# Unread products on TensorE in the idle times around the routing stage of a transformer layer

## The chip, the core and the metric

The kernel runs on one core of one Trainium2 chip. The metric is the device time of one execution in microseconds (us), from start to end of the program on that core. The kernel before takes 848.81 us, the median of three runs (846.87, 848.81 and 850.23). TensorE has two clock levels, 1.2 and 2.4 GHz. The profile shows the granted one as a share of the upper level, 0.50 or 1.00 (a mean over a stretch can lie between).

## What is computed

One transformer layer on x of 8 blocks x 512 rows x 256 features, in fp32: attention with 16 heads and a bias by relative position, then a mixture of seven routed experts (two per row) and one shared expert.

```
x = x + attention(layernorm(x))        # softmax(q k / 4 + bias) v, then Wo
y = layernorm(x)
sh = gelu(y @ sw1 + sb1) @ sw2 + sb2
topv, topi = top_k(y @ gate_w.T + expert_bias, 2); w = softmax(topv)
routed = sum over the two chosen e of w_e * (gelu(y @ rw1[e] + rb1[e]) @ rw2[e] + rb2[e])
out = x + sh + routed
```

## The kernel before

The program has three stages, each a block in which every engine has its own list of instructions; a block ends for all engines together. Inside a block the order of each engine's work is written out by hand, and semaphores (`wait_ge`, `then_inc`) tie the engines to each other.

`project` (L254) makes q, k and v of the eight blocks. `attend` (L573) runs 32 slots of four heads each. Its PE list computes scores for the row maxima (L800), exponents (L817, L825) and the values (`values`, L830, products at L839 into `pC`). The last thing that PE does in it is `values` of slot 31 (L860, L861). In the same stage DVE ends with two context products (`context`, L566, L570), which wait for loads of the context and of the inverse denominators and release the output projection through `c_ready`; ACT copies the last `pC` to `ctx_sb` (L775) and SP stores it.

`finish` (L864) has the rest, in three parts. In the routing part (PE: L1647 to L1670) a loop goes over the eight blocks b. `out_projection(b)` (L1520, L1528) makes the attention's output in `pX[:, 1]`, DVE adds the residual (L1134) and takes the statistics, POOL makes the inverse deviation (L1081, L246 to L251), ACT normalises the rows into `xr` (L1411), and PE turns them (`turn_rows`, L1532, L1538), makes the gate product (`gate`, L1544) and turns the logits into `pX[:, 0, 1]` (`turn_logits`, L1550). DVE copies them out (L1156, which counts `lg_done`), chooses the experts and makes ranks and slots (L1221 to L1229) out of `rank`'s products (L1553), and POOL scatters the rows to `routed_rows` by eight indirect DMAs for each block (L1099). Interleaved with this is the shared expert: `shared_up` (L1589), `turn_shares` (L1580), ACT's copy to `cTs` (L1437), `shared_down` (L1602, L1604) and DVE's `add` (L1238). The block of the loop runs b = 0 to 7, and the shared expert of blocks 0 to 4 (`EARLY` is 3) is done by the end of the part.

Between the parts (PE: L1671 to L1683, "the gap" in what follows) DVE works out a table of tiles (L1241), SP writes padding rows (L1021) and, once all scatters have landed, loads the first eight tiles of 256 rows (L1040). PE meanwhile does the shared expert of blocks 3 and 4. In the expert part (L1684 on) PE takes 38 tiles: `turn_tile` (L1614), `expert_up` (L1626), `expert_down` (L1637); DVE scales the results and POOL scatters them (L1115). Then the last three blocks of the shared expert and the sums follow.

`ident` is the 128x128 identity, `wo_f` the output projection's weights in fp32, both in SBUF from before the end of the attention on (`small_ld` counts eight loads, the last of them issued at about 480 us). `pS`, `pU`, `pD` and `pX` are PSUM banks. An fp32 product shows as two records of PE in the trace.

Of the kernel before, what the change touches and what calls it, by code (L numbers as in the profile page):

```python
# [20 lines left out]
B, S, D = 8, 512, 256  # L21
# [4 lines left out]
NI = HG * B  # L26
# [43 lines left out]
SMALL = 8  # L70
# [26 lines left out]
def raw(t):  # L97

    return t.bitcast(F32)
# [10 lines left out]
def layer_kernel(nc, x, wqT, wkT, wvT, woT, rel_emb, gateT, expert_bias, w1, b1, w2, b2, low_rows,  # L110
# [22 lines left out]
    with top:  # L133
# [32 lines left out]
        with ExitStack() as ctx:  # L166

            sb, _, sem = mk(ctx)
            near = sb("near", [P, 2, HPG, TW], F32)
            bandT = sb("bandT", [P, 2, HPG // 2, 2, BW], F32R)  # L170
            q_st = sb("q_st", [P, RING, HPG // 2, S], F32R)
            k_st = sb("k_st", [P, RING, HPG // 2, S], F32R)
            v_raw = sb("v_raw", [P, RING, TT * HPG * DH], F32)
            near_ld = [sem(f"near_loaded{j}") for j in range(HPG)]
            band_ld = [sem(f"band_loaded{j}") for j in range(HPG)]
            qk_ld = [sem(f"qk_loaded{r}") for r in range(RING)]
            far_ld = [sem(f"far_loaded{r}") for r in range(RING)]
            v_ld = [sem(f"v_loaded{r}") for r in range(RING)]
            rows_set = sem("rows_set")
            qk_out = [sem(f"qk_out{m}") for m in range(4)]  # L180
            v_out = sem("v_out")
            loads = attention_loads(locals())
            scope = locals()
            project(nc, mk, scope)
            attend(nc, mk, scope)
# [384 lines left out]
    dve.tensor_tensor(cn[:, b % 2], cn[:, b % 2], rb[:, b % 2], ALU.mult).then_inc(g["c_ready"], 1)  # L570


def attend(nc, mk, g):  # L573


# [6 lines left out]
    with ExitStack() as ctx:  # L582
# [8 lines left out]
        pS = ps("pS", [P, 3, S], F32)  # L591
        pE = ps("pE", [P, 4, S], F32)
        pC = ps("pC", [P, S], F32)
        s_mm, max_done, split_done, max_turned, max_out, max_ld = (sem(n) for n in (
            "s_mm", "max_done", "split_done", "max_turned", "max_out", "max_loaded"))
# [3 lines left out]
        PV0, MAX0 = 8, 4  # L599
# [12 lines left out]
        with nc.Block() as block:  # L612
# [174 lines left out]
            def _(pe):  # L787
# [42 lines left out]
                def values(n, par, t, first=False):  # L830

                    if t == 0:
                        pe.wait_ge(exp_done, STEPS * n + STEPS)
                        pe.wait_ge(v_ready, n + 1)
                        if not first:
                            pe.wait_ge(evac, n)
                    for j in range(HPG):
                        at = 8 * (j // 2) + 2 * t + j % 2
                        ins = pe.matmul(pC[32 * j:32 * j + 32], v_aug[:, par, t, j], prob[:, par, at],  # L839
                                        start=t == 0, stop=t == TT - 1, skip_group_check=True)  # L840
                    ins.then_inc(pv_done, 1)
# [17 lines left out]
                        slot(4 * quad + u, u, quad, first=quad == 0, last=quad == QUADS - 1)  # L859
                for t in range(TT):  # L860
                    values(NI - 1, 1, t)  # L861


def finish(nc, mk, g):  # L864
# [3 lines left out]
    passed, ident = g["passed"], g["ident"]  # L868
    ctx_dram, rden_dram, xs_dram, yc_dram = g["ctx_dram"], g["rden_dram"], g["xs_dram"], g["yc_dram"]
    wst, x1, wo_f, ga_f, eb, b1s, b2f, b2_low, ctx_sb = (  # L870
        g[n] for n in ("wst", "x1", "wo_f", "ga_f", "eb", "b1s", "b2f", "b2_low", "ctx_sb"))
    cn, rb, w_sh, x1c, route = g["cn"], g["rb"], g["w_sh"], g["x1c"], g["route_sb"]
    wst_ld, x_ld, small_ld = g["wst_ld"], g["x_ld"], g["small_ld"]
    c_ready, route_ld, x_late, pad_out = g["c_ready"], g["route_ld"], g["x_late"], g["pad_out"]
    with ExitStack() as ctx:
# [70 lines left out]
        def down_of(b, t2):  # L946
            return pX[:, 0, t2].rearrange("p (u d) -> p u d", u=2) if b == OWN else pD[:, t2]

        def hidden_of(b):
            return cn[:, 0] if b == OWN else h_f  # L950

        def shares_of(b):
            return hT[0:3 * NE, 0, 0] if b == OWN else cTs

        def last_user(b):
            return b - 2 if b > OWN else b - 1
# [17 lines left out]
        pU = ps("pU", [P, 2, S], F32)  # L974
        pD = ps("pD", [P, 2, 2, D], F32)
        pX = ps("pX", [P, 2, 2, S], F32)
# [6 lines left out]
        s = {n: sem(n) for n in names}  # L983
# [11 lines left out]
        with nc.Block() as block:  # L995
# [523 lines left out]
            def _(pe):  # L1519
                def out_projection(b):  # L1520
                    pe.wait_ge(c_ready, b + 1)
                    for t2 in range(2):
                        if b >= 1:
                            pe.wait_ge(s["x1_add"], 2 * b - 1 + t2)
                        for u in range(2):
                            t = 2 * t2 + u
                            for c in range(MC):
                                ins = pe.matmul(pX[:, 1, t2, D * u:D * u + D], cn[:, b % 2, c, t:S:TT], wo_f[:, c],  # L1528
                                                start=c == 0, stop=c == MC - 1)
                        ins.then_inc(s["wo_mm"], 1)  # L1530

                def turn_rows(b):  # L1532
                    pe.wait_ge(s["xn1"], 4 * b + 4)
                    if b >= 1:
                        pe.wait_ge(s["r_done"], b)
                    for c in range(MC):
                        for t in range(TT):
                            ins = pe.transpose(pX[:, 0, c, P * t:P * t + P], xr[:, b % XR, t, 0, P * c:P * c + P], ident[:])  # L1538
                        ins.then_inc(s["xT2_mm"], 1)
# [30 lines left out]
                def turn_shares(b):  # L1570
                    pe.wait_ge(s["comb_done"], 3 * b + 3)
                    if b == TILES_FROM:
                        pe.wait_ge(s["ev_done"], 2 * NT)
                    if b == OWN:
                        pe.wait_ge(s["xlo"], NT)
                    elif b >= 1:
                        pe.wait_ge(s["sh_acc"], 2 * last_user(b) + 2)
                    flat = down_of(b, 1)[0:3 * NE].rearrange("p u d -> p (u d)")
                    for t in range(TT):
                        ins = pe.transpose(flat[:, P * t:P * t + P], raw(combine_p[:, b % CB, t]), ident[:])  # L1580
                    ins.then_inc(s["c_turn"], 1)

                def shared_up(b, m):
                    if b == TILES_FROM:
                        pe.wait_ge(s["hhi"], 2 * NT)
                    if b >= 1 and b != OWN:
                        pe.wait_ge(s["h_done"], 2 * last_user(b) + m + 1)
                    for c in range(MC):
                        ins = pe.matmul(up_of(b, m), w_sh[:, 0, c, P * m:P * m + P], x2T(b)[:, c],  # L1589
                                        start=c == 0, stop=c == MC - 1)  # L1590
                    ins.then_inc(s["u_mm"], 1)

                def shared_down(b, halves=(0, 1)):
                    pe.wait_ge(s["b2_split"], 2)
                    pe.wait_ge(s["h_done"], 2 * b + 2)
                    pe.wait_ge(s["cT_done"], b + 1)
                    if b >= 1 and b != OWN:
                        pe.wait_ge(s["sh_acc"], 2 * last_user(b) + 2)
                    for t2 in halves:
                        for u in range(2):  # L1600
                            t = 2 * t2 + u
                            pe.matmul(down_of(b, t2)[:, u], shares_of(b)[:, P * t:P * t + P], b2s[:], start=True, stop=False)  # L1602
                            for m in range(2):
                                ins = pe.matmul(down_of(b, t2)[:, u], hidden_of(b)[:, m, P * t:P * t + P], w_sh[:, 1, m],  # L1604
                                                start=False, stop=m == 1)
                        ins.then_inc(s["d_mm"], 1)
# [40 lines left out]
                pe.wait_ge(small_ld, 16 * SMALL)  # L1647
                out_projection(0)
                out_projection(1)
                turn_rows(0)  # L1650
                pe.wait_ge(s["consts"], 8 + NE)
                pe.wait_ge(s["tri_done"], 1)
# [21 lines left out]
                pe.matmul(pX[:, 1, 0, 0:2 * NE], ones_b[:], cum[:, B], start=True, stop=True).then_inc(s["cnt_mm"], 1)  # L1674
                shared_up(EARLY + 1, 1)
                shared_down(EARLY)
                turn_shares(EARLY + 1)
                shared_down(EARLY + 1)
                pe.wait_ge(s["tab_done"], 2)
                pe.wait_ge(s["r_done"], B)  # L1680
                pe.wait_ge(s["h_done"], 2 * TILES_FROM)
                pe.wait_ge(s["sh_acc"], 2 * TILES_FROM)
                pe.wait_ge(s["w_lo"], 2 * NR)  # L1683
                experts = ()  # L1684
                for k in range(-3, NT):
                    if k + 3 < NT:
# [110 lines left out]
```

## Time and profile before

| | us |
|---|---|
| median of three runs | 848.81 |
| lowest and highest | 846.87, 850.23 |
| the profiled execution | 853.25 |
| its span, first to last instruction | 851.4 |
| PE busy in it | 785.6 (92%) |
| DVE busy | 620.7 (73%) |
| ACT busy | 477.5 (56%) |
| POOL busy | 252.5 (30%) |
| mean granted clock of TensorE | 0.943 |

The span starts with the first instruction; all times of rows are counted from there. The attention stage ends at about 523 us, the routing part at about 655, the gap at about 678, the expert part at about 812. Matmuls are pipelined, so the last record of a group overlaps the next group by some tenths of a microsecond. "Idle before" in a timeline stands in square brackets with what ended it.

### The profile page before, as it was taken

Reading aid. Unit: us, or ns where it says so; the run is one execution under the profiler, and the core shown is the slowest. Engines: PE = TensorE matmul, PEld = TensorE weight load, DVE = VectorE, ACT = ScalarE, POOL = GpSimd, SP = SyncE. Lnnn points to the kernel's source line nnn. Section 1 sums busy time; section 2 is a strip of 40 time slices with the busy share of each in tenths; the row PEclk is TensorE's granted clock in tenths of the full one; section 3 lists DMA queues with packets and bytes.
Section 4 is the critical chain, followed back from the end, with each engine's and each line's share of the span. In section 5 each row is a group of like instructions: output and inputs, shape, how many; then the busy total and the mean of one; then the engine's idle time right before and its main releaser. Section 6 shows DMA issues by size and latency. Waiting matters only on the chain. (4 is left out here: it accounts for less than half of the span.)

```text
span 851.4 us, 18147 instructions
## 1 busy us (share of the span) xinstructions
PE 785.6 (92%) x6177; PEld 543.4 (64%) x6177; DVE 620.7 (73%) x1928; ACT 477.5 (56%) x720; POOL 252.5 (30%) x407
## 2 busy tenths in 40 slices
PE   4999889999999999999999997688878799999996
PEld 2777646666666666666656555455553499999954
DVE  5666588888888888888888832576765367667854
ACT  2444306666666666666666672465553177777720
POOL 1122011111121112111211110277776145655530
PEclk9999959999999999999999998699898689999998
DMA  4999894543564335443444813455513625556676
GB/s 118 279 350 355 281 221 106 161 116 94 131 167 133 95 106 169 131 117 114 125 138 135 278 61 126 153 185 181 165 71 101 189 84 150 168 158 206 199 259 235
DMA packets 74631, 140.75 MB, mean 165 GB/s; under 512 B 14520, under 2 KB 34640, under 8 KB 74366
## 3 DMA queue, kind: packets, MB, share of 16 engines
q1 hardware_dynamic: 62962, 116.91, 45.7%
q0 software_dynamic: 9792, 19.54, 7.0%
q10 hardware_dynamic: 1788, 3.18, 1.1%
q8 instruction: 49, 0.80, 0.4%
q14 instruction: 40, 0.33, 0.1%
HBM read 85.71 MB, written 56.78 MB: 167 GB/s over the span
## 5 line engine op out<-in xcount | busy, mean ns | idle before, releaser
L734 DVE CUSTOM_DVE_ANT_0 sums<-pS,near 128x512 bf16<-128x512 f32 x512 | 329.4, 687 | 47.7 <-PE pS L800 39.0
L767 ACT ACTIVATE prob<-pE 128x1024 f32<-128x1024 f32 x256 | 248.4, 1022 | 148.3 <-PE pE L825 148.3
L825 PEld LDWEIGHTS pE<-bandT,place 64*128 64x128 f32 x2048 | 166.1, 189 | 12.6
L825 PE MATMUL pE<-bandT,place 64*128 64x244 f32 (+2 forms) x2048 | 163.3, 271 | 0.0
L800 PE MATMUL pS<-k_st,q_st 48*128 48x512 f32 x512 | 138.3, 476 | 6.1 <-DMA k_st<-k_parts 3.5
L839 PE MATMUL pC<-prob,v_aug 128*32 128x512 f32 x1024 | 135.7, 604 | 1.0 <-ACT ctx_sb L775 1.0
L800 PEld LDWEIGHTS pS<-k_st,q_st 48*128 48x128 f32 x512 | 62.6, 192 | 115.2 <-DVE nmax L734 88.3
L817 PE MATMUL pE<-q_st,k_st 62*128 62x512 f32 x512 | 114.9, 406 | 2.0 <-issue 1.9
L1115 POOL DMA_INDIRECT expert_rows<-rb,xr x76 | 77.3, 1017 | 75.9 <-DVE rb L1328 61.3
L1099 POOL DMA_INDIRECT routed_rows<-xr,slot_i x64 | 65.2, 1019 | 33.4 <-issue 19.3
L1637 PE MATMUL pD<-w2p,hT 128*128 x456 | 63.8, 289 | 2.0 <-DVE hT L1321 1.6
L817 PEld LDWEIGHTS pE<-q_st,k_st 62*128 62x128 f32 x512 | 57.1, 188 | 8.4 <-ACT prob L767 5.0
L703 POOL DMA_DIRECT2D q_st<-negated_maxima x64 | 34.8, 548 | 91.2 <-DMA negated_maxima<-turned 91.2
L1637 PEld LDWEIGHTS pD<-w2p,hT 128*128 128x128 f32 x456 | 56.8, 190 | 2.9 <-issue 2.9
L712 POOL COPY v_aug<-v_raw 128x256 f32<-128x256 f32 x32 | 12.6, 395 | 151.9 <-PE pC L839 151.9
L498 PE MATMUL pQ<-xT,w_p 128*128 128x512 f32 x192 | 49.8, 410 | 2.6 <-DVE xT L409 1.5
L696 POOL DMA_DIRECT2D negated_maxima<-turned x32 | 22.5, 703 | 90.0 <-DVE turned L747 86.0
L1321 DVE TENSOR_TENSOR hT<-ctx_sb,hT 128x512 fp32r<-128x512 f32 x38 | 26.3, 693 | 27.8 <-ACT hT L1467 21.8
L498 PEld LDWEIGHTS pQ<-xT,w_p 128*128 128x128 f32 x192 | 36.2, 196 | 14.0 <-DVE qk L416 4.5
L1604 PE MATMUL pD<-w_sh,ctx_sb 128*128 128x256 f32 x112 | 44.8, 539 | 0.0
L734 DVE DVE_READ_ACCUMULATOR2_ANT nmax<- 128x1 f32 x512 | 42.5, 83 | 0.0
L839 PEld LDWEIGHTS pC<-prob,v_aug 128*32 128x32 f32 x1024 | 20.6, 108 | 32.7 <-issue 30.0
(187 smaller groups left out, 1046.8 us busy)
## 6 DMA issues: line engine op xcount, KB each, us to landing
xr<-routed_rows SPq DMA_DIRECT2D x38, 258.0 KB
q_st<-q_parts SPq DMA_DIRECT2D x64, 128.0 KB, 2.7
k_st<-k_parts SPq DMA_DIRECT2D x64, 128.0 KB, 2.9
ctx<-ctx_sb SPq DMA_DIRECT2D x32, 256.0 KB, 2.8
q_parts<-qk SPq DMA_DIRECT2D x14, 512.0 KB, 8.2
k_parts<-qk SPq DMA_DIRECT2D x14, 512.0 KB, 7.6
near<-bias_by_distance SPq DMA_DIRECT2D x16, 448.0 KB, 5.0
xr<-expert_rows SPq DMA_DIRECT2D x14, 512.0 KB, 6.6
```

The costliest lines, as they stand in the source:

```text
L498: ins = pe.matmul(pQ[:, m % 2], w_p[:, a, w, c, P * h:P * h + P], xT[:, par, z, c], start=k == 0, stop=k == 5)
L703: pool.dma_start(raw(q_st[row:row + KM, m % RING]), max_dram[m].rearrange("a (p h) s -> h a p s", h=2)[side]).then_inc(max_ld, 16)
L734: dve.tensor_tensor_reduce(sums[:, r % 4], pS[:, unit % PS], near[:, hg % 2, j, lead:lead + S], -1.0, BIG, ALU.add, ALU.min, nmax[:, j, t: ...
L767: act.activation(prob[:, par, 2 * step:2 * step + 2], pE[:, 2 * (step % 2):2 * (step % 2) + 2], ACT.Exp).then_inc(exp_done, 1)
L800: pe.matmul(pS[:, unit % PS], q_st[rows, r, pair, P * t:P * t + P], k_st[rows, r, pair], start=True, stop=True).then_inc(s_mm, 1)
L817: pe.matmul(pE[:, bank + side], k_st[rows, r, pair, P * t:P * t + P], q_st[rows, r, pair], start=True, stop=False, skip_group_check=True)
L825: ins = pe.matmul(pE[:, bank + side, a:z], place[rows, half], bandT[rows, (quad // 2) % 2, pair, part, lead:lead + z - a], start=False, st ...
L839: ins = pe.matmul(pC[32 * j:32 * j + 32], v_aug[:, par, t, j], prob[:, par, at], start=t == 0, stop=t == TT - 1, skip_group_check=True)
L1099: pool.indirect_dma_start(xs_dram[:, :], bass.IndirectOffsetOnAxis(ap=slot_i[:, b, c, t:t + 1], axis=0), xr[:, b % XR, t, c], None).then_i ...
L1115: pool.indirect_dma_start(yc_dram[:, :], bass.IndirectOffsetOnAxis(ap=place_of, axis=0), y_rows(i)[:, t], None).then_inc(y_out[i % NXG], 16)
L1604: ins = pe.matmul(down_of(b, t2)[:, u], hidden_of(b)[:, m, P * t:P * t + P], w_sh[:, 1, m], start=False, stop=m == 1)
L1637: ins = pe.matmul(pD[:, i % 2, t], hT[:, i % 2, a, TS * m + P * t:TS * m + P * t + P], w2p[:, bass.ds(expert, 1), z, m].rearrange("p a n - ...
```

## The change

A helper `keep_turning` issues `count` fp32 products of `ident` with the first 256 columns of `wo_f` into a given PSUM bank. Nothing reads the results, and no semaphore is counted by them. It is called at five places of PE's list: after the last `values` of the attention (five products into `pS`, behind two waits of its own), after `out_projection(1)` (six into `pU`), after `shared_down(EARLY)` (two into `pX[:, 0, 1]`, behind a wait on `lg_done`), after `turn_shares(EARLY + 1)` (four into the same bank), and behind the waits that stand ahead of the expert part (three into `pU`). Twenty products in all. Nothing is removed or moved.

```diff
@@ -570,6 +570,12 @@
     dve.tensor_tensor(cn[:, b % 2], cn[:, b % 2], rb[:, b % 2], ALU.mult).then_inc(g["c_ready"], 1)
 
 
+def keep_turning(pe, g, bank, count):
+
+    for _ in range(count):
+        pe.matmul(bank, g["ident"][:], g["wo_f"][:, 0], start=True, stop=True)
+
+
 def attend(nc, mk, g):
 
 
@@ -859,6 +865,9 @@
                         slot(4 * quad + u, u, quad, first=quad == 0, last=quad == QUADS - 1)
                 for t in range(TT):
                     values(NI - 1, 1, t)
+                pe.wait_ge(g["small_ld"], 16 * SMALL)
+                pe.wait_ge(max_done, MAX0 + 16 * NI)
+                keep_turning(pe, g, pS[:, 0, 0:D], 5)
 
 
 def finish(nc, mk, g):
@@ -1647,6 +1656,7 @@
                 pe.wait_ge(small_ld, 16 * SMALL)
                 out_projection(0)
                 out_projection(1)
+                keep_turning(pe, g, pU[:, 0, 0:D], 6)
                 turn_rows(0)
                 pe.wait_ge(s["consts"], 8 + NE)
                 pe.wait_ge(s["tri_done"], 1)
@@ -1674,13 +1684,17 @@
                 pe.matmul(pX[:, 1, 0, 0:2 * NE], ones_b[:], cum[:, B], start=True, stop=True).then_inc(s["cnt_mm"], 1)
                 shared_up(EARLY + 1, 1)
                 shared_down(EARLY)
+                pe.wait_ge(s["lg_done"], B)
+                keep_turning(pe, g, pX[:, 0, 1, 0:D], 2)
                 turn_shares(EARLY + 1)
+                keep_turning(pe, g, pX[:, 0, 1, 0:D], 4)
                 shared_down(EARLY + 1)
                 pe.wait_ge(s["tab_done"], 2)
                 pe.wait_ge(s["r_done"], B)
                 pe.wait_ge(s["h_done"], 2 * TILES_FROM)
                 pe.wait_ge(s["sh_acc"], 2 * TILES_FROM)
                 pe.wait_ge(s["w_lo"], 2 * NR)
+                keep_turning(pe, g, pU[:, 0, 0:D], 3)
                 experts = ()
                 for k in range(-3, NT):
                     if k + 3 < NT:
```

## Rows read from the trace of the kernel before

**Rows 1.** The head of the page.
```profile
span 851.4 us, 18147 instructions
```

**Rows 2.** Stretches: start:end, length, busy time of five engines, granted clock, DMA.
```profile
519.70:522.40 2.70, 0.00 (x0) 0.00 (x0) 0.54 (x1) 0.57 (x1) 0.00 (x0) 1.00 0.60 228
522.50:529.20 6.70, 5.64 (x13) 4.60 (x14) 1.28 (x2) 0.00 (x0) 1.17 (x16) 0.50 0.07 20
...
536.20:549.70 13.50, 10.12 (x26) 5.69 (x27) 8.42 (x43) 7.78 (x16) 2.48 (x8) 0.50 0.56 176
...
638.60:645.20 6.60, 6.60 (x13) 3.06 (x14) 2.58 (x4) 3.58 (x8) 5.08 (x6) 0.50 0.32 115
...
665.90:686.20 20.30, 17.18 (x52) 12.57 (x53) 4.72 (x9) 5.42 (x11) 0.00 (x0) 0.50 0.50 140
```

**Rows 3.** Timeline of PE, 515 to 552: start, duration, instructions, idle before, releaser.
```profile
515.98 3.64 PE L839 MATMUL pC<-prob,v_aug 128*32 128x512 f32 x32 [0.98 <-ACT ctx_sb L775]
523.56 10.28 PE L1528 MATMUL pX<-wo_f,cn 128*128 128x256 f32 x32 [3.94 <-PEq L612]
538.04 1.97 PE L1538 MATMUL pX<-ident,xr 128*128 128x128 f32 x8 [4.20 <-ACT xr L1411]
540.78 3.57 PE L1544 MATMUL pX<-x2T,ga_f 128*7 128x512 f32 x4 [0.78 <-ACT x2T L1419]
...
545.64 5.83 PE L1528 MATMUL pX<-wo_f,cn 128*128 128x256 f32 x16
```

**Rows 4.** Timeline of PE, later groups of the same lines.
```profile
560.14 4.00 PE L1528 MATMUL pX<-wo_f,cn 128*128 128x256 f32 x16
...
566.47 1.88 PE L1544 MATMUL pX<-x2T,ga_f 128*7 128x512 f32 x4 [0.74 <-ACT x2T L1419]
...
625.44 1.06 PE L1538 MATMUL pX<-ident,xr 128*128 128x128 f32 x8 [0.41 <-DVE ranks L1221]
...
637.41 1.09 PE L1538 MATMUL pX<-ident,xr 128*128 128x128 f32 x8 [1.85 <-ACT xr L1411]
```

**Rows 5.** Timeline of DVE, 516 to 531.
```profile
521.86 1.23 DVE L570 TENSOR_TENSOR cn<-cn,rb 128x1024 f32<-128x1024 f32 x1 [4.04 <-DMA rb<-inverse_denominators]
...
530.14 0.69 DVE L1134 TENSOR_TENSOR x<-pX,x 128x512 f32<-128x512 f32 x1 [2.01 <-PE pX L1528]
```

**Rows 6.** Timeline of POOL, its first indirect DMA of the routing part.
```profile
553.58 1.20 POOL L1099 DMA_INDIRECT routed_rows<-xr,slot_i  x1 [7.77 <-DVE slot_i L1229]
```

**Rows 7.** Timeline of PE, 657 to 689.
```profile
657.32 0.38 PE L1602 MATMUL pD<-b2s,cTs 24*128 24x256 f32 x1
...
661.75 1.13 PE L1604 MATMUL pD<-w_sh,ctx_sb 128*128 128x256 f32 x4
664.40 0.60 PE L1580 MATMUL pD<-ident,combine_p 128*24 128x128 f32 x4 [1.52 <-DVE x1c L1238]
667.36 0.55 PE L1602 MATMUL pD<-b2s,cTs 24*128 24x256 f32 x1 [2.36 <-ACT cTs L1437]
...
675.38 2.08 PE L1604 MATMUL pD<-w_sh,ctx_sb 128*128 128x256 f32 x4
678.55 1.94 PE L1614 MATMUL pX<-ident,xr 128*128 128x128 f32 x8 [1.09 <-DVE x1c L1238]
681.05 2.93 PE L1626 MATMUL pU<-xgT,w1c 128*128 128x256 f32 x12 [0.56 <-DVE xgT L1306]
...
687.16 1.67 PE L1637 MATMUL pD<-w2p,hT 128*128 x12
```

**Rows 8.** Timelines of ACT, DVE and the SP queue, 660 to 681.
```profile
666.52 0.59 ACT L1437 ACTIVATE cTs<-pD 24x512 fp32r<-24x512 f32 x1 [1.63 <-remote]
...
677.50 0.69 DVE L1238 TENSOR_TENSOR x1c<-pD,x1c 128x512 f32<-128x512 f32 x1 [4.26 <-PE pD L1604]
...
672.48 8.12 SPq L1040 DMA_DIRECT2D xr<-routed_rows  x8
```

**Rows 9.** DMA issues of the whole run: count, KB each, median us to landing.
```profile
out<-x1d SPq DMA_DIRECT2D x2, 256.0 KB, 2.0
```

## The prediction, made before the changed kernel ran

> **What bounds the kernel now.** I read the page first, then the granted clock of TensorE by stretches, then PE's timeline in the stretches at half clock, then the timelines of the engines that release PE there.
>
> The span is 851.4 us [rows 1], and PE is the busiest engine in nearly all of it, so its clock matters wherever PE is what comes late. The stretches [rows 2] show when it doesn't run at 2.4 GHz. The last values of the attention end at 519.62, PE stands idle for 3.94 us until the projection at 523.56 [rows 3], and the clock, still 1.00 up to 522.4, is at 0.50 (1.2 GHz) from 522.5 to 529.2. After the two projections PE stands for 4.20 us [rows 3], and the clock is at 0.50 again from 536.2 to 549.7. Between the last sums of the shared expert of block 3 (662.88) and those of block 4 (667.36) PE does only 0.60 us of transposes [rows 7], and the clock is at 0.50 from 665.9 to 686.2. These three pieces hold 40 us at half clock, and the five additions stand in the idle times ahead of, or inside, these pieces. There are other short pieces at half clock, such as 638.6 to 645.2 [rows 2], that nothing of the change touches.
>
> Is PE late in these pieces? From 523.56 on the chain goes projection(0), DVE's sum at 530.14 [rows 5], statistics, POOL's and ACT's normalising, transposes at 538.04, gate product at 540.78, logits, projection(2) to 551.5 [rows 3], ranks, slots, and POOL's first indirect DMA at 553.58, for which it had waited 7.77 us [rows 6]. From there on POOL issues its scatters nearly without rest, so what moves its first one moves the whole routing part; I find nothing in it that hangs on a fixed time, since the context loads, weight loads and scatters are all released from this same chain. In the third piece the shared sums run from 667.36 to 677.46, DVE adds them, and only then does PE turn the first tile, at 678.55 [rows 7, 8].
>
> **The change, part by part.** A product here is the form of the projection: 128x128 stationary, 256 columns, fp32. Its group of 16 records (8 products) takes 4.00 us at full clock [rows 4], so one costs 0.50 us. At half clock 13 records take 5.64 us of busy time [rows 2], 0.87 us a product, and the two products at 675.38 take 2.08 us [rows 7], 1.04 each: 0.87 to 1.04.
>
> Place 1, five products after the attention: 2.5 us, from 519.62 to 522.1. The block can't end before DVE's second context product, 521.86 + 1.23 = 523.09 [rows 5], so they are hidden with 1.0 us to spare. Their waits are for loads issued some 40 us earlier and for maxima long done. PE's idle time shrinks from 3.94 to 1.4 us, and the clock should be full at 523.56. Then projection(0) takes 4.00 us and ends at 527.56 where DVE's sum started at 530.14: 2.6 us gained on the chain.
>
> Place 2, six products after the two projections: these now end at 523.56 + 8.00 = 531.6, and the six at 534.6. The transposes, which wait for ACT, come at 538.04 - 2.6 = 535.4, so the six are hidden with 0.8 us to spare. If the clock stays full, three groups of the chain shorten: transposes 1.97 to 1.06, gate 3.57 to 1.88, projection(2) 5.83 to 4.00 [rows 3, 4], in all 0.9 + 1.7 + 1.8 = 4.4 us. Places 1 and 2 together: 7.0 us, POOL's first scatter at 546.6. What is late next there is DVE's choosing of the experts, which ends before projection(2) and so hides under it.
>
> Here a rule can be weighed. The trace has groups of transposes that differ in the idle time ahead: at 625.44, after 0.41 us of idle, the clock didn't fall; at 637.41, after 1.85 us, it was at 0.50 from 638.6 [rows 2, 4]. In the changed kernel the idle ahead is 0.8, between the two. The Trainium skill (TensorE: Matmul & The Clock Gate, Part 4: PE-mode transpose) says that transposes don't count as busy in the way products do. By that rule the stretch from 534.6 to the gate product is idle as a whole, and the time would be that of the first rival. The row at 625.44 neither shows nor excludes it.
>
> Place 3, two products after the shared sums of block 3: 662.88 to 663.9. The transposes behind them wait for DVE until 664.40 [rows 7]; hidden with 0.5 us to spare. The added wait on the logits' copy is long fulfilled, as all routing is behind it. Place 4, four products behind these transposes: 665.0 to 667.0, while PE stands until 667.36 for ACT's copy at 666.52 [rows 7, 8]; hidden with 0.4 us to spare. ACT's 1.63 us of idle before that copy has no releaser that I can name. If it were absent in some run, the four products would be late by up to 1 us. With the clock kept, the shared sums of block 4 take as long as those of block 3 did, 657.32 to 662.88, 5.56 us in place of 10.1, and end at 672.9.
>
> Place 5, three products, 1.5 us, behind the last waits and directly ahead of the first tile's transposes. The waits were fulfilled 1.09 us after the sums; now that is 674.0, and the three end at 675.5. Is a tile there by then? SP issues the first tile load at 672.48 [rows 8], and transfers of 256 KB land after 2.0 us [rows 9], with seven more queued behind this one and the last scatters just done: 674.5 at the earliest, and 676 if it takes as much again. So the load covers most of the 1.5 us, and without that cover they would cost their full 1.5. The transposes start at 675.5 to 676, in place of 678.55: 3.0 us. The filling of the expert pipeline, 678.55 to 687.16, then runs at full clock: halving 1.94, 2.93 and the following transposes and products (3.3 us until the first down product) [rows 7] gives up to 4.1 us; but ACT's and DVE's steps between these groups don't shorten, and start to show. I take 2.6, with 2.0 and 3.1 as bounds. Places 3 to 5: 5.6 us.
>
> The sum is 7.0 + 5.6 = 12.6 us. The profiled execution took 853.25 us around its span of 851.4; less 12.6 that is 840.6. The median of the runs is 848.81, 4.4 lower than the profiled one, and 848.81 - 12.6 = 836.2. I don't take all of it: the profiled one may hold more time at half clock than the others, for where the clock rises and falls varies. The piece from 665.9 to 686.2 is the likeliest to be shorter elsewhere, since PE was busy in 17.18 of its 20.3 us [rows 2] before the clock rose. I take 2 us off the gain for this and predict 838 us. Past 690 nothing is changed, and the work there hangs on the tiles' progress, so I let the gain reach the end.
>
> **The rivals.** First, the clock is held in only one of the two places. If it falls again around the first transposes, 4.4 us of 12.6 are lost; if in the third piece, 5.6: by the same scaling 838 + 4.4 = 842.4 and 843.6. For it: the stretch between 534.6 and the gate product has 0.8 + 1.06 + 0.78 us with no product. Against: a similar stretch at 625.44 stayed at full clock. Chance 0.25.
>
> Second, the gain is swallowed: POOL's scatters, the loads of context or the expert phase's DMAs turn out to set the end, or an earlier schedule puts the unchanged short idles of the routing part so that the clock falls there more often. Each such piece of 6.6 us at half clock costs up to 3.3 us [rows 2]; three more eat 10: 845 to 852. Against it speaks POOL's wait of 7.77 us before its first scatter. Chance 0.08. That the change doesn't do what it says (products that keep nothing up, yet fit under the waits) gives 848.8: chance 0.03.
>
> Third, slower: the products don't hold the clock, and then cost double just where they stand ahead of waited-for work. At 0.87 to 1.04 us each: five end at 524.0 to 524.8 against 523.56 (0.4 to 1.3 late); six after 533.84 at 539.1 to 540.1 against 538.04 (1.0 to 2.0); two and four 0.3 to 0.6 and 1.1 to 1.9; three ahead of the first tile 2.6 to 3.1. Sum 5.4 to 8.9, so some 856 us. It decides from where the clock is at 0.50 at 523.56 in spite of five products. Against it: at each fall in these rows PE had hardly any product in the 3 us before. Chance 0.04.
>
> **How the numbers follow.** Forecast 838 (834 to 841) 0.60; one place only 0.25; swallowed 0.08; no effect 0.03; slower 0.04. A measurement of this kernel can tell about 0.5%, 4.2 us, from no change: the bounds are 844.6 and 853.1. The first two cases lie below 844.6 but for a tail of 0.02, and most of the swallowed case above it: faster 0.84, same 0.12, slower 0.04. The range takes the forecast's full scaling with the upper bounds of the unknowns (848.8 - 12.6 - 2.5 = 833.7) with 1 us for run-to-run spread below, and the one-place case with a little of the swallowed one above: 833 to 845.
>
> **What would show it.** Granted clock 1.00 from 523 to 550 in the profile after; PE's idle ahead of the projection near 1.4 us with its start still near 523.6; POOL's first scatter near 546.6; shared sums of block 4 in 5.6 us; first tile transposes 3 us after SP's first tile load. A start of the projection later than 523.6, transposes that no longer wait for ACT or DVE, or a clock of 0.50 at these places would prove the step wrong.

## The result

The changed kernel takes 840.05 us, the median of 15 runs (833.45 to 846.43), against 846.87 us for the kernel before in 15 runs (840.16 to 850.54). The ratio is 0.9906, with a 95% interval of 0.9879 to 0.9933: 8.0 us faster, between 5.7 and 10.2. Measured once more on another occasion (below) it was 0.9875 (0.9841 to 0.9910). The forecast was 838 us, 10.8 us below the 848.81 us known then. Ratios, intervals and the means over many runs leave out executions more than 1.5% above the fastest of the same kernel.

The head of the page after, its line of the clock in 40 slices, and the stretches (columns as in [rows 2]):

```profile
span 835.4 us, 18227 instructions
...
PEclk9999959999999999999998999998998999999999
```
```profile
521.00:523.30 2.30, 2.30 (x12) 1.76 (x10) 0.00 (x0) 0.60 (x1) 0.00 (x0) 1.00 0.68 257
525.30:538.00 12.70, 11.07 (x50) 10.39 (x51) 7.16 (x21) 2.09 (x5) 3.39 (x23) 1.00 0.49 128
539.10:542.30 3.20, 3.09 (x4) 0.38 (x4) 1.27 (x2) 1.92 (x4) 1.04 (x2) 0.50 0.56 205
664.00:690.00 26.00, 23.51 (x164) 20.63 (x164) 12.60 (x25) 14.73 (x34) 5.24 (x5) 1.00 0.46 135
```

The projections and the whole third piece run at full clock now, where [rows 2] had 0.50. One short fall is left near the first gate product, 3.4 us in place of the 13.7 us of before. (Lengths of falls are read from the clock's own record; the stretches shown stay some tenths inside them.) PE's timeline at the start of the routing part, against [rows 3]; line numbers are 6 to 10 higher than before, and L576 is the added product:

```profile
520.94 2.43 PE L576 MATMUL pS<-wo_f,ident 128*128 128x256 f32 x10
525.26 7.81 PE L1537 MATMUL pX<-wo_f,cn 128*128 128x256 f32 x32 [1.90 <-PEq L618]
532.91 2.75 PE L576 MATMUL pU<-wo_f,ident 128*128 128x256 f32 x12
537.29 1.09 PE L1547 MATMUL pX<-ident,xr 128*128 128x128 f32 x8 [1.63 <-ACT xr L1420]
539.21 3.46 PE L1553 MATMUL pX<-x2T,ga_f 128*7 128x512 f32 x4 [0.83 <-ACT x2T L1428]
...
543.78 4.11 PE L1537 MATMUL pX<-wo_f,cn 128*128 128x256 f32 x16
```

The five products end 1.90 us before the projection may start, the six end 1.63 us before the transposes may: both hidden. The projections take 7.81 us in place of 10.28. The gate product came at half clock here, 3.46 us. PE had stood 1.63 and 0.83 us on both sides of the transposes; but in e1 below it stood 1.61 and 0.83 us at the same place and the clock stayed up, so these idle times alone don't decide it. In the gap, against [rows 7]:

```profile
660.19 1.03 PE L576 MATMUL pX<-wo_f,ident 128*128 128x256 f32 x4
661.81 0.60 PE L1589 MATMUL pD<-ident,combine_p 128*24 128x128 f32 x4 [0.59 <-issue]
662.24 1.89 PE L576 MATMUL pX<-wo_f,ident 128*128 128x256 f32 x8
664.88 0.35 PE L1611 MATMUL pD<-b2s,cTs 24*128 24x256 f32 x1 [0.74 <-ACT cTs L1446]
...
669.28 1.13 PE L1613 MATMUL pD<-w_sh,ctx_sb 128*128 128x256 f32 x4
671.39 1.53 PE L576 MATMUL pU<-wo_f,ident 128*128 128x256 f32 x6 [0.99 <-DVE x1c L1247]
672.76 0.60 PE L1623 MATMUL pX<-ident,xr 128*128 128x128 f32 x4
673.74 0.66 PE L1623 MATMUL pX<-ident,xr 128*128 128x128 f32 x4 [0.37 <-DMA xr<-routed_rows]
...
678.53 1.67 PE L1646 MATMUL pD<-w2p,hT 128*128 x12
```

The shared sums of block 4 run from 664.88 to 670.41, 5.53 us in place of 10.1, and the second half of the first tile's transposes waits 0.37 us for a DMA: in this trace the loads have become what is late. It isn't so in every trace (e9 below).

### The profile page after: what moved, and what is told of

It is laid out like the page before. It is cut to its first block and busy times, and to the rows that moved or that the text cites. A ratio compares the mean times of both kernels' runs of the same rounds, so it can differ in the third digit from the quotient of the medians.

```text
span 835.4 us, 18227 instructions
## 1 busy us (share of the span) xinstructions
PE 777.1 (93%) x6217; PEld 540.0 (65%) x6217; DVE 619.8 (74%) x1928; ACT 478.5 (57%) x720; POOL 254.1 (30%) x407
## 5 line engine op out<-in xcount | busy, mean ns | idle before, releaser
L449 ACT ACTIVATE qk<-pQ 128x512 fp32r<-128x512 f32 x32 | 19.2, 599 | 32.0 <-PE pQ L498 25.7
```

## Landmarks of all kernels

The two profiled executions differ by 16.0 us, twice the gain of 8.0 us, so they can't be compared end to end. The attention also ends at different times (the projection starts at 523.6 to 532.6 in these traces). So I read the same landmarks from PE's, DVE's, POOL's and SP's timelines of each kernel, counted from the start of the first projection. "Load to down" goes from SP's first tile load to PE's first down product of the experts, "rest" from there to the end; the last column sums the time at half clock from 516 us on, by the clock's record. All are one execution each, in us.

| kernel | DVE's second sum | first scatter | count product | sums of block 4 | load to down | rest | at half clock |
|---|---|---|---|---|---|---|---|
| before | 6.58 | 30.02 | 131.82 | 10.10 | 14.68 | 164.24 | 70 |
| after | 4.12 | 24.79 | 127.60 | 5.53 | 9.07 | 156.87 | 20 |
| e1, places 1 and 2 | 4.11 | 23.18 | 123.86 | 8.60 | 10.58 | 164.69 | 27 |
| e2, places 3 to 5 | 5.39 | 26.99 | 127.49 | 5.56 | 9.49 | 160.14 | 28 |
| e3, 8 columns wide | 6.44 | 29.82 | 128.30 | 8.62 | 15.75 | 162.14 | 48 |
| e4, no place 5 | 4.12 | 24.55 | 124.05 | 5.52 | 10.22 | 161.29 | 27 |
| e5, as transposes | 5.63 | 26.11 | 127.16 | 5.56 | 12.02 | 158.17 | 29 |
| e6, doubled | 4.11 | 23.94 | 126.67 | 5.55 | 11.52 | 159.51 | 24 |
| e7, place 1 | 5.64 | 28.97 | 129.83 | 7.44 | 12.95 | 156.40 | 45 |
| e8, more places | 4.12 | 23.19 | 122.49 | 5.55 | 11.64 | 163.78 | 17 |
| e9, the change again | 4.11 | 24.78 | 126.33 | 5.56 | 11.35 | 160.40 | 31 |
| e10, at the seams | 5.30 | 24.38 | 124.66 | 5.52 | 9.02 | 157.11 | 18 |

The column "rest" holds nothing that any of these kernels changes but three products of e8, and it spreads over 8 us. The profiled execution after was 7.4 us better in it than the one before. That doesn't go with the products: e7, with nothing at places 2 to 5, has 156.40 and e1 164.69. The other columns hold what the change does, but scatter too: e2 has nothing at places 1 and 2, and its first scatter still came 3.0 us sooner than before's. So single differences against the trace before are upper ends, and averages over several traces are better.

## Experiments

My theory: the products hold the clock in two pieces, about 7 us in the first (places 1 and 2) and 5 to 6 us in the gap (places 3 to 5), and cost nothing as each place is covered by a wait. Rivals: only one piece gives; the added waits or the shifted instructions do it and not the clock; place 5 is on the path; POOL's scatters set the pace, so that the clock doesn't matter in the middle of the routing part; transposes don't hold the clock. The edits are to the changed kernel; ratios are to the kernel before on the same chip, with 95% intervals.

**Each part alone.** e1 leaves out places 3 to 5:

```diff
-                pe.wait_ge(s["lg_done"], B)
-                keep_turning(pe, g, pX[:, 0, 1, 0:D], 2)
...
-                keep_turning(pe, g, pX[:, 0, 1, 0:D], 4)
...
-                keep_turning(pe, g, pU[:, 0, 0:D], 3)
```

> Places 1 and 2 alone (five products after the attention, six after the two projections). By the theory that the clock is held at both pieces and each gives its share, the profile has granted clock 1.00 at the two projections, a first scatter 5 to 7 us earlier after the start of the projection, and still 0.50 in the shared sums of block 4; the time is 3 to 6 us below the kernel before (ratio 0.993 to 0.9965). By the rival that only the last three places give anything, the ratio is 0.998 to 1.002.

Measured: 0.9916 (0.9878 to 0.9953), a little more gain than the 0.993 to 0.9965 expected, which the interval reaches. The first scatter came 23.18 us after the projection's start, 6.8 us sooner than before, with no fall of the clock at the gate product this time. The stretches of e1:

```profile
527.90:536.00 8.10, 8.06 (x34) 8.04 (x35) 3.85 (x12) 0.00 (x0) 2.30 (x17) 1.00 0.21 65
...
663.90:670.60 6.70, 6.58 (x14) 4.10 (x15) 0.69 (x1) 0.00 (x0) 0.00 (x0) 0.50 0.40 92
670.80:679.50 8.70, 6.63 (x47) 5.51 (x47) 3.84 (x8) 4.75 (x11) 0.00 (x0) 1.00 0.77 228
```

The last two lines matter for my sum: without places 3 to 5 the clock falls in the gap here too, but it was back after 6.8 us, not after the 20.5 us of the trace before. The shared sums took 8.60 us, and the filling of the expert pipeline ran at full clock.

e2 leaves out places 1 and 2 instead:

```diff
-                pe.wait_ge(g["small_ld"], 16 * SMALL)
-                pe.wait_ge(max_done, MAX0 + 16 * NI)
-                keep_turning(pe, g, pS[:, 0, 0:D], 5)
...
-                keep_turning(pe, g, pU[:, 0, 0:D], 6)
```

> Places 3, 4 and 5 alone. By the theory the shared sums of block 4 take 5.6 us in place of 10.1, the first down product of the expert part comes 5 us earlier relative to the first tile load's chain, and the time is 3 to 6 us below the kernel before (ratio 0.993 to 0.9965); together with the first two places the two gains add up to the 8 us of the whole change. By the rival that the loads of the first tiles set this piece anyway, the ratio is 0.998 to 1.002.

Measured: 0.9950 (0.9912 to 0.9988). Its stretches, the falls at the projection and at the first gate product, and the gap:

```profile
528.00:531.40 3.40, 3.04 (x7) 2.56 (x8) 0.00 (x0) 0.00 (x0) 1.17 (x16) 0.50 0.13 39
541.70:548.40 6.70, 5.49 (x12) 1.90 (x12) 3.04 (x5) 3.54 (x7) 1.70 (x5) 0.50 0.63 176
660.00:684.00 24.00, 19.95 (x109) 15.22 (x108) 9.85 (x22) 8.25 (x18) 4.25 (x5) 1.00 0.65 186
```

So both pieces give, 7.1 and 4.2 us as measured, and the rival of one piece only is out, though e2's interval ends only just below 1. The first two falls were shorter here, 3.4 and 6.8 us, than the 6.8 and 13.7 us of before, with the same code up to that point: their price varies from one execution to the next.

**The clock or something else.** e3 keeps all places, waits and instructions, but makes the products 8 columns wide:

```diff
-        pe.matmul(bank, g["ident"][:], g["wo_f"][:, 0], start=True, stop=True)
+        pe.matmul(bank[:, 0:8], g["ident"][:], g["wo_f"][:, 0, 0:8], start=True, stop=True)
```

> The same twenty products at the same five places with the same added waits, but 8 columns wide in place of 256, so PE stands idle as before. By the theory (it is the clock) everything is as in the kernel before: clock 0.50 at the projections and in the shared sums of block 4, ratio 0.998 to 1.002. By the rival that the added waits or the shifted instructions change the schedule whatever the clock does, part of the gain remains: ratio below 0.996.

Measured: 0.9995 (0.9961 to 1.0030). The stretches of e3:

```profile
526.00:532.70 6.70, 5.31 (x13) 4.29 (x14) 1.52 (x2) 0.00 (x0) 1.18 (x16) 0.50 0.08 21
539.60:553.20 13.60, 9.91 (x25) 5.59 (x26) 8.53 (x42) 8.08 (x16) 2.49 (x8) 0.50 0.60 181
669.40:676.00 6.60, 6.60 (x14) 4.09 (x15) 0.69 (x1) 0.00 (x0) 0.00 (x0) 0.50 0.46 122
```

All three pieces fall again, and the time is that of the kernel before. Over its runs the mean granted clock is 0.954, as in the kernel before on the same chip (0.953), against 0.965 in e1 and e4. The gain is the clock's, not that of waits or of the place of instructions.

**Place 5.** e4 leaves out the three products ahead of the first tile (the last line of e1's diff).

> Places 1 to 4 without the three products ahead of the first tile. By the theory these three are covered by the load of the first tile, which the transposes wait for: the first transposes come within 0.3 us of where they come with them, and the ratio to the kernel before is that of the whole change, 0.988 to 0.993, with the clock at risk of falling once in the filling of the expert pipeline. By the rival that they are on the path, this kernel is up to 1.4 us faster than the whole change.

Measured: 0.9868 (0.9812 to 0.9924). PE's timeline and a stretch:

```profile
672.07 0.63 PE L1623 MATMUL pX<-ident,xr 128*128 128x128 f32 x4 [2.22 <-DMA xr<-routed_rows]
673.64 0.66 PE L1623 MATMUL pX<-ident,xr 128*128 128x128 f32 x4 [0.94 <-DMA xr<-routed_rows]
674.12 2.69 PE L1635 MATMUL pU<-xgT,w1c 128*128 128x256 f32 x12
```
```profile
674.50:677.80 3.30, 3.30 (x17) 3.30 (x17) 0.69 (x1) 2.65 (x7) 0.00 (x0) 0.50 0.81 234
```

PE waits 2.22 us for the first tile, where the three products would stand: in this trace they would be covered. Without them the clock fell for 3.4 us in the filling, and load to down was 10.22 us, against 9.07 after and 9.49 in e2, but 11.35 in e9, which has the products. Both effects are too small for the times: the intervals of e4 and of the whole change overlap widely.

The cover is not there in every trace. PE's and SP's timelines in e9, the changed kernel itself:

```profile
671.85 1.13 PE L1613 MATMUL pD<-w_sh,ctx_sb 128*128 128x256 f32 x4
673.97 1.53 PE L576 MATMUL pU<-wo_f,ident 128*128 128x256 f32 x6 [0.99 <-DVE x1c L1247]
675.34 1.04 PE L1623 MATMUL pX<-ident,xr 128*128 128x128 f32 x8
```
```profile
669.75 8.13 SPq L1049 DMA_DIRECT2D xr<-routed_rows  x8
```

The shared sums ended 3.2 us after the first tile load was issued, not 0.7 us as in e4. All eight transposes follow the products without any wait for a DMA, though in e4 the first tile was usable 2.88 us after the issue. By that the tile was in at about 672.6, an estimate, and the three products held the transposes up by the 1.4 us from 673.97 to 675.34. It is the same in e5, e6 and e8. So place 5 is covered in part where the sums end soon after the load is issued (after, e2, e10), and costs up to 1.4 us elsewhere. No run tells what it is worth on the whole.

**Transposes in place of products.** e5 issues four 128x128 transposes for each product:

```diff
-    for _ in range(count):
-        pe.matmul(bank, g["ident"][:], g["wo_f"][:, 0], start=True, stop=True)
+    for k in range(8 * count // 2):
+        pe.transpose(bank[:, P * (k % 2):P * (k % 2) + P], g["wo_f"][:, 0, P * (k % 2):P * (k % 2) + P], g["ident"][:])
```

> At all five places each product is replaced by four 128x128 transposes, which take about the same 0.5 us of PE. By the theory that the clock goes by PE being at work, transposes too, it stays at 1.00 at the two projections and in the shared sums of block 4, and the ratio is 0.988 to 0.993. By the rival rule that transposes don't count as busy, the clock is 0.50 in both pieces as in the kernel before, and the transposes themselves cost what they stand in the way: ratio 0.999 to 1.006.

Measured: 0.9881 (0.9811 to 0.9951). In the gap, PE's timeline and the stretch:

```profile
664.71 0.60 PE L1589 MATMUL pD<-ident,combine_p 128*24 128x128 f32 x4 [1.84 <-DVE x1c L1247]
665.14 1.91 PE L576 MATMUL pX<-ident,wo_f 128*128 128x128 f32 x16
666.98 0.38 PE L1611 MATMUL pD<-b2s,cTs 24*128 24x256 f32 x1
```
```profile
527.00:530.20 3.20, 3.20 (x9) 2.48 (x9) 0.69 (x1) 0.00 (x0) 0.00 (x0) 0.50 0.13 39
...
656.70:690.00 33.30, 29.50 (x199) 25.00 (x199) 16.42 (x37) 14.27 (x31) 8.87 (x9) 1.00 0.51 148
```

Between 662.0 and 667.0 PE did nothing but 1.84 us of idling and transposes, and the clock stayed at 1.00, where in the four traces with nothing at places 3 to 5 or only narrow products (before, e1, e3, e7) it fell each time. The rule of the Trainium skill (TensorE: Matmul & The Clock Gate, Part 4: PE-mode transpose), that transposes don't count as busy in the way products do, doesn't hold for these fp32 transposes, as far as holding a clock that is already up goes; no run shows whether they can raise it. Place 2 agrees: the fall after it was 3.4 us long in e5, as in after, e4 and e9, and 13.7 us in before, e3 and e7 (6.8 in e2). So do the other runs, though e5 has only four: their mean granted clock is 0.970, against 0.955 in the kernel before on the same chip. At place 1 the clock fell in e5, at 526.9, with PE standing 2.73 us there; with products it fell in e7 after 2.02 us and in e10 after 4.20 us, and stayed up in e8 after 2.83 us. That place tells nothing apart.

**How large the covers are.** e6 doubles every count (10, 12, 4, 8, 6).

> Twice as many products at every place (10, 12, 4, 8, 6). By the theory that each place is covered by a wait with the slack read from the trace (about 1.4, 1.6, 0.6, 0.7 us, and the load of the first tile) the doubled ones stick out by what is left: 2.4 - 1.4 = 1.0 us at the first, 2.8 - 1.6 = 1.2 at the second, 0.4 at the third, 1.2 at the fourth, 1.3 at the fifth, so the time is 4 to 5 us above that of the whole change (ratio to before 0.994 to 0.998). By the rival that the cover is far larger (DMA sets the pace), it is within 1 us of the whole change.

Measured: 0.9933 (0.9897 to 0.9969), some 2 to 5 us above the whole change, though the intervals overlap; 4 to 5 us and 0.994 to 0.998 were expected. PE's timeline in e6:

```profile
538.03 5.34 PE L576 MATMUL pU<-wo_f,ident 128*128 128x256 f32 x24
543.22 1.04 PE L1547 MATMUL pX<-ident,xr 128*128 128x128 f32 x8
...
666.77 3.62 PE L576 MATMUL pX<-wo_f,ident 128*128 128x256 f32 x16
670.32 0.38 PE L1611 MATMUL pD<-b2s,cTs 24*128 24x256 f32 x1
```

At places 2 and 4 the doubled products run straight into the work that follows, without idle in between; at place 2 the transposes come 12.83 us after the projection's start in place of 12.03. At place 1 even ten products left 0.80 us of idle, as the projection waited longer for its loads in this trace. So the covers are real, and they end between one and two times the counts of the change.

**Place 1 alone.** e7 leaves out places 2 to 5.

> Place 1 alone. By the theory only the two projections run at full clock: DVE's second sum comes 2.6 us sooner after the start of the projection, the clock falls again before the first gate product, and the gain is 2 to 3 us (ratio 0.9965 to 0.998). By the rival that place 1 carries the whole gain of the first part, this is as fast as places 1 and 2 together.

Measured: 0.9969 (0.9927 to 1.0012). The stretches:

```profile
528.40:531.60 3.20, 3.20 (x9) 2.54 (x9) 0.69 (x1) 0.00 (x0) 0.00 (x0) 0.50 0.15 41
538.70:552.10 13.40, 9.77 (x25) 5.44 (x26) 8.35 (x41) 8.03 (x16) 2.48 (x8) 0.50 0.62 183
```

The clock fell for 3.4 us in the projection in spite of the products, so DVE's second sum came 0.9 us sooner and not the 2.6 us expected; it fell again before the gate product, as expected. The first scatter is only 1.0 us sooner than before. The size fits, though the interval doesn't exclude nothing at all.

**More of the same, and where it matters.** e8 adds products at six further waits of the routing part and two at the end, and two at place 2:

```diff
-                keep_turning(pe, g, pU[:, 0, 0:D], 6)
+                keep_turning(pe, g, pU[:, 0, 0:D], 8)
...
+                    if i % 2 == 0:
+                        keep_turning(pe, g, pX[:, 0, 1, 0:D], 3 if i else 1)
                     turn_logits(i)
...
+                    if i in (2, B - 2):
+                        pe.wait_ge(s["lg_done"], i + 1)
+                        keep_turning(pe, g, pX[:, 0, 1, 0:D], 3 if i == 2 else 4)
                     if i + 1 < B:
                         turn_rows(i + 1)
...
+                keep_turning(pe, g, pX[:, 1, 0, 0:D], 2)
                 turn_shares(B - 1)
+                keep_turning(pe, g, pX[:, 1, 0, 0:D], 1)
                 shared_down(B - 1)
```

> The whole change with more of the same: eight products in place of six after the projections, one before the logits' transposes of block 0 and three before those of blocks 2, 4 and 6, three and four before the row transposes of blocks 3 and 7, and two and one at the last shared sums. By the theory each of the remaining pieces at half clock in the routing part (four of 3 to 7 us in the kernel before, three in the changed one) costs half its length where PE is late, so 2 to 5 us more are gained: ratio 0.983 to 0.989. By the rival that POOL's scatters set the routing part's pace once it has begun, the clock is at 1.00 nearly throughout and the time is within 1 us of the whole change.

Measured: 0.9892 (0.9849 to 0.9935), not clearly better than the whole change (0.9906 and 0.9875). The stretches, and PE at the count product:

```profile
527.00:651.70 124.70, 106.08 (x462) 70.21 (x460) 82.63 (x393) 63.47 (x123) 79.59 (x136) 1.00 0.44 145
651.90:658.50 6.60, 5.48 (x9) 2.54 (x10) 5.75 (x29) 0.00 (x0) 4.62 (x5) 0.50 0.46 135
```
```profile
653.02 0.20 PE L1689 MATMUL pX<-cum,ones_b 128*128 128x16 bf16 x1 [4.70 <-DVE cum L1223]
```

Nearly the whole routing part, up to 651.8, ran at full clock, and yet from the first scatter to the count product it took 99.3 us, where the kernels with 10 to 24 us at half clock in it took 98.5 to 102.8. PE was early at its end and waited 4.70 us for DVE. Once the scatters have begun, POOL and DVE set the pace in these traces, and falls of PE's clock are hidden there. The 2 to 5 us more that I expected don't show, and the rival fits; the interval still reaches into the expected range. A third reading isn't tested: that the clock gave something and the 22 further products, where they stand ahead of work, took it back.

**Again, and at the seams.** e9 is the changed kernel itself. e10 adds products only where the clock should matter, ahead of the first scatter and behind the last ranks:

```diff
-                keep_turning(pe, g, pU[:, 0, 0:D], 6)
+                keep_turning(pe, g, pU[:, 0, 0:D], 8)
...
+                    if i == 0:
+                        keep_turning(pe, g, pX[:, 0, 1, 0:D], 1)
                     turn_logits(i)
...
+                    if i == B - 1:
+                        pe.wait_ge(s["lg_done"], B)
+                        keep_turning(pe, g, pX[:, 0, 1, 0:D], 2)
                     rank(i)
...
                 shared_up(EARLY + 1, 0)
+                keep_turning(pe, g, pX[:, 0, 1, 0:D], 1)
                 pe.wait_ge(s["tab_chain"], 3 * B)
```

> The whole change once more, beside the next kernel on one chip. By the theory that its two parts simply add and that the rest is scatter between runs, the ratio to the kernel before is 0.986 to 0.993 and the profile's granted clock is 1.00 in the shared sums of block 4 again, with at most one short fall around the first gate product. By the rival that the whole is less than the sum of its parts (7.1 and 4.2 us as measured alone), it stays at 0.990 to 0.995.

> The whole change plus products only at the places that decide two falls: eight in place of six after the projections, one before the first logits' transposes, two before the ranks of block 7 and one before the count product. By the theory falls in the middle of the routing part are hidden by POOL's scatters, and only those before its first scatter and after its last rank count: the first scatter comes 23.2 us after the projection's start, the count product and the shared sums of block 4 stay at clock 1.00, and the time is 1 to 2 us below the whole change. By the rival that these too are within what DMA hides, it equals the whole change within 0.5 us; if the products hold up the ranks or the count, it is slower by up to 1 us.

Measured: e9 0.9875 (0.9841 to 0.9910), e10 0.9861 (0.9803 to 0.9919), medians 839.27 and 836.59 us. The whole gives 8.0 and 10.6 us in its two measurements, and its parts 7.1 and 4.2 us, 11.3 in sum. The intervals hold both simple addition and a whole somewhat less than its parts; e9 lies in the range expected for addition. Whether e10 is faster still stays open, as the intervals overlap. Its first scatter came after 24.38 us, not the 23.2 expected, and its trace shows a weak spot of place 1. DVE's timeline and the stretches of e10:

```profile
530.94 1.23 DVE L570 TENSOR_TENSOR cn<-cn,rb 128x1024 f32<-128x1024 f32 x1 [5.60 <-DMA rb<-inverse_denominators]
```
```profile
526.00:532.00 6.00, 2.44 (x14) 1.82 (x10) 1.06 (x1) 0.60 (x1) 0.00 (x0) 1.00 0.53 167
532.20:535.50 3.30, 2.86 (x7) 2.35 (x8) 0.00 (x0) 0.00 (x0) 1.18 (x16) 0.50 0.15 40
```

The load of the inverse denominators came later than usual, PE stood 4.20 us after the five products, and the clock fell in spite of them.

## Why the prediction was right, and where its sizes were off

**The mechanism** held: products at full clock in waits, clock kept, chain shortened (e3 shows that it is the clock). Two of its steps held only in some traces, the clock at the first gate product and the cover of place 5.

**Place 1**: predicted DVE's second sum 2.6 us sooner, measured 2.46 (6.58 to 4.12) against the trace before; but e2, without the products, has 5.39, and in e7 and e10 the clock fell in spite of them. **Place 2**: hidden with 1.63 us to spare, predicted 0.8. The first scatter was forecast 7.0 us sooner than in the trace before; it came 6.8 sooner in e1, but 5.2 to 5.5 in the traces after, e4 and e9, each of which had one short fall at the first gate product. That fall was the first rival's mechanism, at a smaller price than its 4.4 us, about 1.6 us of first scatter, since the clock was back after 3.4 us, in time for most of projection(2) (4.11 us). The prediction weighed by idle times whether the clock would fall there; with nearly the same ones it stayed up in e1 and fell in the other three. The forecast also took the trace before as the usual case, and it is the latest of all. The first scatter came after 28.95 us on average in the four traces that lack place 1, place 2 or both or have them narrow (before, e2, e3, e7), and after 24.33 us in the four with both at the counts of the change (after, e1, e4, e9): 4.6 us sooner. The count product follows with 3.9 us. "What moves POOL's first scatter moves the whole routing part" held within the scatter of the traces: first scatter to count product 98.5 to 102.8 us in all of them.

**Places 3 and 4**: shared sums of block 4 forecast at 5.56 us, measured 5.52 to 5.56 in all eight kernels that have something at both places. **Place 5**: forecast to be mostly covered by the first tile load. That is so in the trace after and by e4's 2.22 us of waiting, and not in e9.

**The terms that were mis-sized** are the gains of both parts, 7.0 and 5.6 us, for one reason: they were taken against one profiled execution that held more half-clock time than the others. In its gap the clock stayed low for 20.5 us; in e3, e7 and e1, with nothing that holds the clock in the gap, it was low for 17, 13.7 and 6.8 us of it. Load to down averages 13.5 us over these three and before, and 9.7 us over after, e2, e9 and e10: 3.8 us (3.4 with e8, whose gap has the same products). With 4.6 us for the first part that makes 8.0 to 8.4, and the two measurements say 8.0 and, from 0.9875, 10.6. I took 2 us off the sum for just this reason, and some 4 us by these averages would have been the size. The range, 833 to 845, holds both medians.

The clock also goes with the distance between the profiled execution and the median. Over 56 runs of the kernel before, the mean granted clock is 0.953 at 847.8 us, and each 0.01 of clock goes with 5.5 us; the profiled one had 0.943 and 853.25 us. Over 25 runs of the changed kernel it is 0.967 at 839.2 us: 0.014 more clock, worth 7.7 us by that slope, and 8.6 us less time. The slope is a fit over runs on more than one chip, not a price measured by itself.

**The rivals**: "swallowed" is true of the middle of the routing part (e8), but not of its ends, where the change acts. "Slower" is out (its two products of place 3 at half clock would have been 0.2 to 0.6 us late by its own prices, not 0.3 to 0.6). e6 shows what products cost that stick out of their cover with the clock up: six more at place 2 delayed the transposes by 0.8 us, less than their 3 us.

## What to carry to other kernels

Where TensorE waits for another engine for 3 to 4 us and is itself late afterwards, some products that nobody reads, just fewer than the wait holds, keep its clock up and save the half-clock time that would follow, here 8 us for twenty products. Check the wait in more than one trace: at place 5 it was there in some executions and not in others. Put them only at waits ahead of stretches where TensorE sets the pace; in a stretch paced by another engine (here POOL's scatters) the clock is free to fall. One trace shows one course of the clock: before pricing such a change, compare the profiled run's clock with that of the other runs, for the trace may show more than the usual loss, as here in both parts.

## What was not expected of the hardware

After a fall the clock came back at very different times in the same code, the shared sums of block 4. In e1, with PE busy in 6.58 of 6.7 us, it was back after 6.8 us. In the kernel before PE was busy without a break for ten microseconds, and the clock stayed low to the end of them and beyond, 20.5 us in all:

```profile
667.40:677.40 10.00, 10.00 (x20) 5.78 (x20) 0.69 (x1) 0.00 (x0) 0.00 (x0) 0.50 0.54 137
```

No run shows why. And fp32 transposes, with short idle times between them, held it up through a wait (e5). The expert part and what follows, untouched by all kernels but e8, took 156.4 to 164.7 us from one execution to the next, as much spread as the effect under study.
